# A four-stage transformer kernel on one core: experts' shares brought by DMA, keys dealt by GpSimd inside the attention, and a keys-values matrix with its mean taken off

## The reference

```
q = silu(q); k = softmax(k, axis=rows)
kv  = einsum('bhnd,bhne->bhde', k, v)          # per head, 16x16
out = einsum('bhnd,bhde->bhne', q, kv)
out = (out - mean(out)) * rsqrt(var(out) + 1e-5) * ln_g + ln_b
out = out * sigmoid(gate(x)) @ w_out.T + b_out
```

## Time and profile before

| | us |
|---|---|
| median of 3 runs (4761.22 to 4762.66) | 4761.25 |
| the profiled execution, its own time | 4765.43 |
| its span, first to last instruction | 4763.8 |
| PE busy (94% of the span) | 4494.4 |
| DVE busy (75%) | 3549.6 |
| ACT busy (66%) | 3149.2 |
| POOL busy (11%) | 543.8 |

### The profile page before, as it was taken

The page is one execution under the profiler, slowest core; times in us unless marked ns, Lnnn a source line. Parts: engine busy times, 40 slices in busy tenths (PEclk is TensorE's granted clock), DMA queues, the critical chain, the costliest instruction groups (busy, mean ns, idle before and its releaser), DMA issues. The chain is left out here.

```text
span 4763.8 us, 109195 instructions
## 1 busy us (share of the span) xinstructions
PE 4494.4 (94%) x37027; PEld 2754.6 (58%) x37027; DVE 3549.6 (75%) x3659; ACT 3149.2 (66%) x5605; POOL 543.8 (11%) x1384
## 2 busy tenths in 40 slices
PE   6599999999999999999999969999886799999999
PEld 5344444444444444444444447777665688888887
DVE  4599999999999999999999955555344554444444
ACT  3168888888888888888888844444474454444444
POOL 4411111111111111111111100000000000000000
PEclk8789999999999999999999979999998899999999
DMA  5520200200202002013121220000001300000000
GB/s 194 177 33 18 33 19 18 35 18 18 35 19 34 18 20 37 19 23 75 40 57 37 45 99 27 27 27 18 27 18 62 112 14 14 9 13 13 13 9 10
DMA packets 217987, 182.45 MB, mean 38 GB/s; under 512 B 128032, under 2 KB 167632, under 8 KB 216448
## 3 DMA queue, kind: packets, MB, share of 16 engines
q1 hardware_dynamic: 201152, 167.99, 13.9%
q0 software_dynamic: 16384, 8.42, 0.7%
HBM read 120.47 MB, written 71.89 MB: 40 GB/s over the span
## 5 line engine op out<-in xcount | busy, mean ns | idle before, releaser
L908 DVE TENSOR_REDUCE PM<-A 128x2 f32<-128x1024 f32 x2092 | 2457.0, 1221 | 90.0 <-PE A L795 58.3
L885 ACT ACTIVATE PR<-SB 128x512 f32<-128x512 f32 x4100 | 2120.7, 603 | 360.9 <-PE SB L808 353.4
L828 PE MATMUL PV<-PR,VH 128*32 128x256 f32 x16384 | 1292.5, 387 | 0.0
L795 PE MATMUL A<-QST,KA 48*128 48x512 f32 x4184 | 1193.5, 476 | 66.2 <-DMA QF<-QFD 40.5
L828 PEld LDWEIGHTS PV<-PR,VH 128*32 128x32 f32 x16384 | 432.3, 110 | 553.5 <-issue 363.4
L795 PEld LDWEIGHTS A<-QST,KA 48*128 48x128 f32 x4184 | 426.6, 187 | 525.7 <-issue 453.5
L808 PE MATMUL SB<-KST,QST 50*128 50x512 f32 x3075 | 687.4, 410 | 4.5 <-issue 4.3
L808 PEld LDWEIGHTS SB<-KST,QST 50*128 50x128 f32 x3075 | 387.1, 187 | 211.5 <-ACT PR L885 202.7
L2068 DVE TENSOR_TENSOR m_h_lo<-m_h_full,m_h_hi 128x512 fp32r<-128x512 f32 x320 | 221.8, 693 | 276.4 <-ACT m_h_hi L1968 276.2
L816 PE MATMUL SB<-KF,QF 99*32 99x512 bf16 x4100 | 414.6, 384 | 1.2 <-ACT PR L885 1.2
L1962 ACT ACTIVATE m_h_full<-m_h,constants 128x512 f32<-128x512 f32 x320 | 219.7, 687 | 275.4 <-PE m_h L69 274.4
(11 more groups left out here) (295 smaller groups left out, 5412.2 us busy)
## 6 DMA issues: line engine op xcount, KB each, us to landing
...
```

Of the source, the lines that this page charges most:

```text
L795: return nc.tensor.matmul(A[:, u % 2 * 2 + e, :], keys, QST[rows, slot, j * TB:(j + 1) * TB], start=True, stop=True)
L828: mm = nc.tensor.matmul(PV[at:at + 2 * HD, 0:HB], VH[:, slot, e, c, :], PR[:, (2 * c + e) % P_SLOTS, b * HB:(b + 1) * HB], start=(c == 0), ...
L885: nc.scalar.activation(PR[:, v % P_SLOTS, :], SB[:, s_bank(v), :], ACT.Exp, scale=SCALE).then_inc(s_free, 1)
L908: nc.vector.tensor_reduce(PM[:, par, :, i, j:j + 1], A[:, u % 2 * 2:u % 2 * 2 + 2, :], AX.X, ALU.max).then_inc(a_free, 1)
```

## The change

- First projections: POOL deals nothing, `dealt`, `KAD` and its stores are gone. POOL fills `QF` and `QST`, which are now allocated outside both phases, with ones at the start of this phase. DVE doesn't fill them in the attention.
- First attention: `KA` isn't loaded. POOL waits for the loaded `KST` of two blocks ahead and copies it into `KA` in the dealt order, two copies of 48 rows per step, at the start of its step. PE waits for `ka_ready`.
- Second projections: DVE takes the keys' maximum of the block (128 x 2 x 512) after the second half of the values.
- Keys-values: the exponentials come in four parts of 1024 columns for each half, transposes start after the first part, four PSUM banks, DVE copies three of four pairs and ACT one, and the multiplication of a pair of key tiles follows two pairs after its transposes. The mean over all 256 outputs is taken off each row of the matrix, which is now 256 x 256 in place of two blocks of 128 x 128.
- Output stage: queries are multiplied with the full matrix (`project3`, 12 matmuls a slot in place of 6); mean and centring are gone; ACT copies the product and squares it, both from PSUM.
- MoE: the selection matrices, the matmul that spreads the shares, and `m_h_full` are gone. DVE copies the transposed shares to SBUF, POOL stores them to DRAM (`CW`), waits, and loads each expert's share row onto 64 partitions, two transfers per chunk into three slots. Silu and the share product work in place in PSUM, on three banks. The router's steps stand one chunk earlier. The output is transposed in two halves through one bank.

The diff, cut to its core:

```diff
-                def deal(half, i, slot, c):
-                    pool.wait_ge(low_ready, count(i * 4 + (c + 1)))
-                    pool.wait_ge(dealt_stored[slot], count(half * 32))
-                    alone(pool, pool_passed)
-                    for j in range(PARTS):
-                        nc.gpsimd.tensor_copy(dealt[slot][:, c - 2, j, :].bitcast(F32).rearrange("p (i q) -> p i q", i=TT),
-                                              parts[slot][:, c, j, :].bitcast(F32).rearrange("p (q i) -> p i q", i=TT)
-                                              ).then_inc(dealt_ready, 1)
-
                 def blocks(half, i, slot, following):
                     fine_parts(half, i, slot, 0, 1)
-                    deal(half, i, slot, 2)
-                    deal(half, i, slot, 3)
                     fine_parts(half, i, slot, 1, 3)
 
                 pool.sem_inc(summed, 4)
-                pool.sem_inc(dealt_ready, 2 * KC * PARTS)
+                nc.gpsimd.memset(QF[:, :, :], 1.0)
+                nc.gpsimd.memset(QST[:, :, :].bitcast(F32), 1.0)
...
+                def deal(b, slot):
+
+                    for e in range(2):
+                        rows = slice(e * HALF, e * HALF + STACK)
+                        nc.gpsimd.tensor_copy(KA[rows, slot, :].rearrange("p (i q) -> p i q", i=TT),
+                                              KST[rows, slot, :].rearrange("p (q i) -> p i q", i=TT)
+                                              ).then_inc(ka_ready, 1)
+                        pool.wait_ge(ka_ready, count(b * 2 + (e + 1)))
+                        alone(pool, passed)
...
+                    pair = HPAIRS - 2 + hp if two is None else two * 2 + hp
+                    block = hp * NB + nb + 2
+                    turns = (HPAIRS // 2 - 1 if two is None else two) * 4 + (block // K_SLOTS + 1)
+                    pool.wait_ge(k_loaded[block % K_SLOTS], count(turns * K_LOAD))
+                    alone(pool, passed)
+                    deal(t + 2, block % K_SLOTS)
...
+                for b in range(2):
+                    pool.wait_ge(k_loaded[b], count(K_LOAD))
+                    deal(b, b)
...
+                    dve.wait_ge(qk_ready, count(i * 4 + 4))
+                    nc.vector.tensor_reduce(R["k_max"][:, :, ds(i, 1)], R["K1"][:, :, ds(i, TB)], AX.X, ALU.max)
...
+                dve.wait_ge(exp_ready, 4 * KC)
+                nc.vector.tensor_reduce(total[:, :], totals[:, :, :], AX.X, ALU.add).then_inc(total_ready, 1)
+                dve.wait_ge(total_ready, 1)
...
+                dve.wait_ge(full_ready, KC)
+                nc.vector.tensor_reduce(row_sum[:, :], kv_full[:, :, :], AX.X, ALU.add).then_inc(summed, 1)
+                dve.wait_ge(summed, 1)
+                nc.vector.tensor_scalar(row_mean[:, :], row_sum[:, :], 1.0 / D, None, ALU.mult).then_inc(averaged, 1)
+                dve.wait_ge(averaged, 1)
+                for k in range(KC):
+                    for n in range(KC):
+                        out, mean = kv_centred[:, k, n * P:(n + 1) * P], row_mean[:, k:k + 1]
+                        if n == k:
+                            nc.vector.tensor_scalar(out, kv_full[:, k, :], mean, None, ALU.subtract).then_inc(centred, 1)
+                        else:
+                            nc.vector.tensor_scalar(out, mask[:, :], 0.0, mean, ALU.mult, ALU.subtract
+                                                    ).then_inc(centred, 1)
...
+                act.wait_ge(max_ready, 1)
+                for part in range(4):
+                    for k in range(KC):
+                        keys = R["K1"][:, k, part * QUARTER:(part + 1) * QUARTER]
+                        nc.scalar.activation(keys, keys, ACT.Exp, bias=neg_max[:, k:k + 1],
+                                             accum_out=totals[:, k, part:part + 1]).then_inc(exp_ready, 1)
+                    if part:
+                        copy(part * 4 - 1)
...
+                def multiply(m):
+                    copied(pe, m)
+                    for k in range(KC):
+                        for t in (2 * m, 2 * m + 1):
+                            mm = nc.tensor.matmul(kv_ps[:, k, 0:P], k_tok[:, t, k * P:(k + 1) * P],
+                                                  R["V1"][:, t, k * P:(k + 1) * P],
+                                                  start=(t == 0), stop=(t == MC - 1))
+                    return mm
+
                 for m in range(PAIRS):
-                    if m >= 2:
-                        pe.wait_ge((copied_even, copied_odd)[m % 2], m // 2)
+                    pe.wait_ge(exp_ready, (m // 4 + 1) * KC)
+                    if m >= 4:
+                        copied(pe, m - 4)
                     for a in range(2):
                         for k in range(KC):
                             tok = (2 * m + a) * P
-                            mm = nc.tensor.transpose(turn_ps[:, m % 2, a * D + k * P:a * D + (k + 1) * P],
+                            mm = nc.tensor.transpose(turn_ps[:, m % 4, a * D + k * P:a * D + (k + 1) * P],
                                                      R["K1"][:, k, tok:tok + P], K["ident"][:, :])
                     mm.then_inc(turned, 1)
-                for s in (copied_even, copied_odd):
-                    pe.wait_ge(s, PAIRS // 2)
-                for k in range(KC):
-                    for t in range(MC):
-                        mm = nc.tensor.matmul(kv_ps[:, k, 0:P], k_tok[:, t, k * P:(k + 1) * P],
-                                              R["V1"][:, t, k * P:(k + 1) * P],
-                                              start=(t == 0), stop=(t == MC - 1))
+                    if m >= 2:
+                        multiply(m - 2)
+                multiply(PAIRS - 2)
+                mm = multiply(PAIRS - 1)
...
-                        for k in range(KC):
-                            mm = product3(nc, att_ps[s][:, k, :], [w[:, k, :] for w in R["kv"]],
-                                          [v[:, k, :] for v in q[s]], True, True)
+                        for n in range(KC):
+                            mm = project3(nc, att_ps[s][:, n, :], R["kv"], q[s], slice(n * P, (n + 1) * P))
...
-                        nc.scalar.copy(o[s][:, :, :], att_ps[s][:, :, :]).then_inc(o_ready[s], 1)
+                        act.wait_ge(ln[s].lo_ready, count(i))
+                        nc.scalar.copy(ln[s].xc[:, :, :], att_ps[s][:, :, :]).then_inc(ln[s].centred, 1)
+                        nc.scalar.activation(ln[s].sq[:, :, :], att_ps[s][:, :, :], ACT.Square
+                                             ).then_inc(ln[s].squared, 1)
...
+                    pool.wait_ge(cw_full, count(i + 1))
+                    alone(pool, passed)
+                    pool.dma_start(d["CW"], shares[0:E, 0, :]).then_inc(shares_stored, 16)
+                    pool.wait_ge(shares_stored, i * 16 + 16)
+                    alone(pool, passed)
                     for p in range(PAIRS):
-                        pool.wait_ge(spread, count(i * PAIRS + max(p - 1, 0)))
-                        alone(pool, passed)
-                        nc.gpsimd.tensor_copy(pick_pair[:, p % 2, :, :],
-                                              pick[:, 2 * p:2 * p + 2].unsqueeze(2).to_broadcast([P, 2, EH])
-                                              ).then_inc(picked, 1)
-                        pool.wait_ge(picked, count(i * PAIRS + (p + 1)))
+                        if p >= SHARE_SLOTS:
+                            pool.wait_ge(kept_ready, count(i * PAIRS + (p - SHARE_SLOTS + 1)))
+                            alone(pool, passed)
+                        for e in range(2):
+                            pool.dma_start(shares[e * EH:(e + 1) * EH, p % SHARE_SLOTS, :],
+                                           d["CW"][2 * p + e, :].partition_broadcast(EH)
+                                           ).then_inc(share_loaded[p % SHARE_SLOTS], 16)
...
-                    pe.wait_ge(full_ready, count(i * C + max(c - 1, 0)))
+                    pe.wait_ge(lo_ready, count(i * C + max(c - 2, 0)))
...
-                        pe.wait_ge(kept_ready, count(i * PAIRS + max(p - 1, 0)))
-                        pe.wait_ge(picked, count(i * PAIRS + (p + 1)))
-                        nc.tensor.matmul(c_ps[:, c % 2, :],
-                                         pick_pair[:, p % 2, :, :].rearrange("q a b -> q (a b)"),
-                                         cw[:, :], start=True, stop=True).then_inc(spread, 1)
+                    project3(nc, h_ps[:, c % RING, :], w, ln.cut[0], cols).then_inc(h_done, 1)
...
+                    nc.scalar.activation(h_ps[:, c % RING, :], h_ps[:, c % RING, :], ACT.Silu,
                                          bias=bias).then_inc(full_ready, 1)
...
+                        nc.vector.tensor_copy(shares[0:E, 0, :], turn_ps[0:E, 1, :]).then_inc(cw_full, 1)
...
+                        dve.wait_ge(share_loaded[slot], i * (32 * turns) + 32 * (turn + 1))
```

(3 more changed lines are left out.)

228 lines of the change are left out of this document (103 added, 125 removed).

## The result

Before 4761.24 us (4759.92 to 4762.66), after 4705.58 us (4699.64 to 4712.77), medians of four runs each: ratio 0.9881, interval 0.987 to 0.9892. The range 4665 to 4715 held; the forecast of 4684.7 was 20.9 us too low. That the range held is in part luck: the measured time lies above the 4665 to 4700 that the forecast's own chances gave to it, in the part kept for rivals (b) and (c), and neither of them occurred. Two stages went the wrong way, and others that did better than forecast made up for a part of it. The profiled execution of the changed kernel took 4706.38 us, its span is 4704.8. The changed kernel's runs lie 13 us apart, those of before 3 us; that is part of what had to be explained.

A forecast was written before the change was run, and what follows sets the result against it. MoE bound by TensorE, attention by TensorE and VectorE, keys-values and output stages by chains of short operations. 54 + 7 + 2.7 - 5.7 + 8.5 + 10 = 76.5 us off the median 4761.25 gave 4684.7; range 4665 to 4715.

The forecast's parts named there:

- (b): MoE: first share late, both transfers at 4.1 us, stall 3.3 us per block in place of 1.0, 4703 us; 15%.
- (c): Second attention: PE clock falls in the new gaps, keys-values and output stage give half, 4694 us; 12%.
- Removed matmuls and waits 63.3: MoE: share-spreading matmuls gone, 58.9 us, and PE's wait before each block's first, 4.4 us; together 63.3 us saved.
- The first share's chain: MoE block head: copy, store, load, product and low part, ending 4024.5 where PE wants it at 4024.3; stall 0.2 us.
- the 1.0 us per block: MoE: PE's stall for each block's first share, taken as 1.0 us, 8 us in all, range 0 to 26.
- (a): MoE: POOL's share transfers become the bound, issue growing with rows to 1.95 us, 230 us more, 4970 us; 11%.
- Without deals: ... 173.3, 5.2 us earlier: First projections, last block: POOL without deals ends its fine parts at 173.3 instead of 178.6, 5.2 us earlier.
- the slow subtraction: First projections: deals slow a DVE subtraction, 2.60 us against 1.22; up to 0.5 us per block on the layernorm chain.
- I cost it at nothing: Attention: POOL's dealing of one key block per step, 2.3 us, fits its idle 19.87 us and costs nothing.
- the distance from shift to shift unchanged: Attention: expected sign in the profile, the time between POOL's successive shifts, one per step, stays the same.
- S+29.3: Keys-values: multiplications end 29.3 us after stage start S, where they ended at S+40.6; 8.5 us saved for the stage.
- the step to the first root: Output stage: first root starts 3.1 us earlier per pair of slots, times 3, plus 0.6; 10 us saved.

The follow-up runs named there:

- experiment 6: Changed kernel with each chunk's shares loaded as four transfers of 32 rows instead of two of 64: 4734.21 us, ratio to before 0.9949.
- experiment 4: Changed kernel with TensorE making its 8 transposes per block of the first projections twice: 4683.64 us, ratio to before 0.9832.
- experiment 8: Changed kernel with query loads spread over six steps, first projections' transposes made twice and the keys' maximum later: 4665.19 us, ratio to before 0.9795.
- experiment 1: Changed kernel with the next pair's query loads spread over steps 0 to 5 instead of all in the first: 4675.7 us, ratio to before 0.9814.
- experiment 9: Changed kernel with SP again issuing six 32 KB key loads per block ahead of the others, GpSimd still dealing: 4686.69 us, ratio to before 0.9841.
- experiment 10: Changed kernel with 32 unused TensorE transposes added at the end of the first projections: 4685.65 us, ratio to before 0.9842.
- experiment 11: Changed kernel with 64 unused TensorE transposes added at the end of the first projections: 4682.76 us, ratio to before 0.9834.
- experiment 12: Kernel before with 64 unused TensorE transposes added at the end of the first projections: 4772.22 us against 4762.36 beside it, ratio 1.0019.
- experiment 5: Changed kernel with the second projections' keys' maximum moved behind the next centring and the gate's low part: 4698.71 us, ratio to before 0.9867.

## Why the prediction was right or wrong

**MoE, right, 54 against 55.2.** Removed matmuls and waits 63.3, chunk distance 2.79 and issue near 0.5 (0.52), all as worked out. The first share's chain came out to 0.2 us. The working from rows gave a stall of 0.2 us per block, and so it is in the trace: PE's first matmul behind the wait for that low part starts at 4009.76, 0.47 us after the matmul ahead of it, where 0.23 is the usual distance. The mis-sized term is the 1.0 us per block that was taken in its place. The rest of the 8 us went elsewhere: in the first block PE waits 2.85 us for low parts, and from the first cut to the second it gained 4.1 us. The blocks behind it gained 7.4 to 7.8 us each, where 7.9 less 0.2 was worked out. So the total is right and its place is in part luck. Rival (b) (both transfers at 4.1) didn't occur; loads land in 2.8 us as a median, the 2.6 taken was close. Rival (a), the issue going with the rows, is refuted by experiment 6 and the 0.523 us. The Trainium skill (DMA: Bandwidth & Descriptors, Anatomy of one DMA — SWDGE (gpsimd) path) gave an estimate of 2.3 us for the landing of 128 KB. In the trace the store of the shares took 2.2 to 2.3 us, which agrees, but the 512 loads 2.6 to 4.2, none as little as 2.3. By that sum, without a stall, the stage would have been 62 us shorter, and it was 55.

**First projections, wrong, -7 against +1.7.** The step "Without deals: ... 173.3, 5.2 us earlier" came out: POOL's work shrank as said (in the last block it waited 3.7 us for DVE), and the last block takes 4.8 us less. The step that failed is that the six blocks ahead of it would keep their length or gain. The gain, through the slow subtraction, was read from one row. It took 2.60 us there and takes 1.84 now, but three more traces with the stage of before have 1.54 to 1.60 at that place, and in the six blocks behind it the mean is 1.72 us before and after. And the clock was left out: PE does a part of each of these blocks at 1.2 GHz, and together they take 7.2 us more. With the clock held up (experiment 4) the stage takes 175.1 us, near the forecast's 176.4. So experiment 4 shows the clock as the cause of the loss, 10.0 us against this trace and 6 to 10 against the others of this code, which took 181.3 to 185.6. The stage of before took 181.6 to 183.4 in three traces. So 1.7 us is one draw, and no gain shows over these draws.

Why the clock falls more often is not shown. In the blocks with a following mean it never fell after a wait of 1.2 us or less (13 blocks, 12 of them in experiments 4 and 8). But the length of the wait doesn't decide alone: after waits of 1.7 to 2.1 us it fell in 42 of 48 blocks with the changed kernel's code (eight traces) and in 3 of 15 with that of before (four traces).

**Attention, wrong, -2.7 against +12.3.** The start is as forecast in kind: the first stretch to the first shift takes 60.7 us against 62.6, 1.9 less for 2.7. "I cost it at nothing" is right for the dealing: POOL has dealt by 590.5 in step 9, and 56 of 64 steps take 38.4 or 38.7 us. The step that failed is one that was never made: of the six KAD loads per key block only the place on SP's queue at the start was counted, and not that in each pair's first step they stood ahead of the query burst. Without them it starts 2.9 us earlier against PE's program, a packet of that program is held back to near the burst's end, and four steps take 0.9 to 6.0 us more, in step 9 3.3 us of standstill and the rest at the lower clock. Shown by experiments 1, 9, 10, 11 and 12. The forecast said "the distance from shift to shift unchanged": this is the sign that gave it away.

**Second attention, right in kind, three sizes off.** Second projections +7.2 for 5.7: six blocks together 6.0 longer where 4.5 was the term. Blocks of 15.3 us, 0.6 longer each as worked out (0.75), stand beside two of 16.5, and those are the ones in which the granted clock fell to 0.90; the forecast had no such term. Experiment 5 shows the place as the cause: it gets 6.3 back. The keys-values stage, timelines of DVE and PE:

```profile
3568.20 0.17 DVE L1504 TENSOR_REDUCE k_neg_max<-k_max 128x2 f32<-128x16 f32 x1 [0.85 <-PEq L107]
...
3571.89 2.82 PE L1578 MATMUL k_turn_ps<-ident,K 128*128 128x128 f32 x12 [6.39 <-ACT K L1552]
...
3592.02 2.84 PE L1566 MATMUL kv_ps<-V,k_tok 128*128 128x128 f32 x24
...
3594.96 0.61 DVE L1520 SCALAR_TENSOR_TENSOR kv_full<-kv_ps,k_rtotal,head_mask 128x128 f32<-128x128 f32 x2 [3.11 <-PE kv_ps L1566]
```

S is 3568.20; transposes begin at S+3.7, as forecast, and the multiplications end at S+26.7, not S+29.3: a pair takes 1.33 us, not 1.46, which is 2.1 us in sixteen, and the half clock at the beginning (0.51 from 3571.9 to 3575.0) cost 1.7 where 2.3 was allowed. The tail grew by 1.6 (2.0 forecast). Output stage: the step to the first root fell as worked out and by somewhat more (timeline of ACT):

```profile
3639.09 0.81 ACT L193 ACTIVATE ln_slot_sq<-att_ps_slot,eps 128x128 f32<-128x128 f32 x2
...
3662.82 0.81 ACT L193 ACTIVATE ln_slot_sq<-att_ps_slot,eps 128x128 f32<-128x128 f32 x2
```

Roots follow each other in 23.7 us, in before in 27.9 (3635.44 to 3663.38). The forecast had 3.1 per pair; 4.2 it was. Rival (c) had the wrong sign.

**Spread of the runs.** Four runs of the changed kernel lie 13 us apart, four of before 3. That would fit stalls that depend on where a fetch meets the burst, but it is not shown: it was not measured run by run, and larger groups of runs of the kernel before, 7 to 15 each, lie 3 to 15 us apart themselves.
